# A fused attention and feed-forward block on one core: where the queries are turned, where an inverse root is taken, and who adds the first groups

## The chip, the cores and the metric

The kernel runs on one NeuronCore of a Trainium2 chip. The metric is the device time of one execution in microseconds (us); lower is better. A core has a matrix engine (TensorE, PE in the rows; its weight loads are PEld), VectorE (DVE), ScalarE (ACT), GpSimd (POOL) and SyncE (SP), which here issues every DMA. The engines run their own instruction streams in order and meet only at semaphores. All DMAs of this kernel are served by the same 16 DMA engines.

## What is computed

```python
x = L0_attn_x                       # (4, 512, 1024) float32: 2048 tokens of 1024
xn = layernorm(x)                   # (x - mean) / sqrt(var + 1e-5)
q, k, v = (xn @ W.T + b).reshape(B, S, 32, 32)        # Wq, Wk, Wv
scores = einsum('bshd,bsgd->bshg', q, k) / sqrt(32)   # head against head, inside a token
scores = where(scores > 0.001, scores, -inf)
attn = softmax(scores) ; ctx = einsum('bshg,bsgd->bshd', attn, v)
x + (ctx @ Wo.T + bo) + ffn(xn)
# ffn: group-scaled int4 weights, gate and up 3584 x 1024, down 1024 x 3584, a scale per 128 inputs
```

Attention is not over the sequence: each token has its own 32 x 32 matrix of scores between its 32 heads.

## The kernel before

**Splitting in two.** Float32 values are held as two float16 parts, HI and LO, and a product is three float16 matmuls (two in the feed-forward part). ScalarE makes the HI part, VectorE or GpSimd the LO part.

**Attention.** The 2048 tokens are 16 tiles of 128. `opening` turns the weights of q, k and v on TensorE and projects tile 0 in between. Then `tile_2(i)` runs for i = 1 to 16 (`TT`). It has 24 quarters. In quarter s, `project(i, s)` does six 128x512 matmuls of tile i (unit s // 4: Q takes units 0 and 1, K 2 and 3, V 4 and 5), and the table `STEPS` hangs other pieces on: S0 to S3 are the scores of tile i-1, X the split of the normed input of tile i+1, V0 to V3 the products with V of tile i-1, and R0 to R3 (`batch`) turn the queries of tile i on TensorE, 32 transposes in four batches of eight, each copied out of PSUM by VectorE or ScalarE (`batch_copy`).

Each engine walks the same quarters in its own order. VectorE's for a tile is: statistics of the next input tile (quarter 0), `layer_norm` (quarter 2), `unit_copy` of unit 0 and `softmax_shift` (quarter 3), `x_part` (4), `unit_copy` of unit 1, mask, sum and division of the softmax (7), and the rest. ScalarE takes the square root of the variance between its copies of S2 and S3 (`ROOT_AT`). SyncE's order, all of it DMAs, is: load the next x, store the context, store V to DRAM (`store_v`), turn V from DRAM (`turn_v`), turn the next x (`turn_x`), turn the probabilities in four pieces (`turn_probs`), store the turned x (`store_xt`), turn K in two halves (`turn_k`).

**The last tile** (i = 16) projects nothing. Its quarters turn Wo on TensorE (`turn_wo`, 16 half rows through PSUM bank 1), start the output projection (`output_unit`, 12 matmuls a quarter into bank 0, emptied by ScalarE's `output_out` before the next), and do the scores and products of tile 15. The other 21 output units follow.

**Feed-forward.** 28 tiles t of 128 rows. A tile has 32 units idx (gate 0 to 15, up 16 to 31; group g = idx // 2 % 8, half = idx % 2), each four 128x512 matmuls into one of three pairs of PSUM banks. ScalarE scales the first group into the sum, VectorE scales and adds the seven others (`add_group`). Down units are woven in from tile 1's second half on.

Of the kernel before, what the change touches and what calls it, by code (L numbers as in the profile page):

```python
# [29 lines left out]
F32 = mybir.dt.float32  # L30
# [11 lines left out]
def build(nc, x_in, Wq, bq, Wk, bk, Wv, bv, Wo, bo, gate_q, gate_s, up_q, up_s, down_q, down_s, out):  # L42
# [24 lines left out]
    ctx_dram = nc.dram_tensor("ctx_scratch", [TT, P, TG, 2, KT, GROUPS], F16).ap()  # L67
    v_dram = nc.dram_tensor("v_scratch", [P, NH * P], F16).ap()
    xt_dram = nc.dram_tensor("xt_scratch", [TT, P, 2, KT, P], F16).ap()

    with ExitStack() as whole:
# [85 lines left out]
        ln_std = sem("ln_std")  # L157
        ln_rstd = sem("ln_rstd")
# [9 lines left out]
        k_turned = [sem(f"k_turned{k}") for k in range(2)]  # L168
        v_stored = sem("v_stored")
        v_turned = sem("v_turned")  # L170
        p_turned = [sem(f"p_turned{k}") for k in range(4)]
        batch_done = sem("batch_done")
        batch_out = [sem("batch_out_act"), sem("batch_out_dve")]
# [29 lines left out]
        gu_added = sem("gu_added")  # L203
        silu_done = sem("silu_done")
# [13 lines left out]
        def anchor(eng):  # L218
# [17 lines left out]
        STATS_AT, ROOT_AT, NORM_AT, SHIFT_AT, EXP_AT, MASK_AT, DIVIDE_AT, P_AT = 0, 2, 2, 3, 5, 7, 7, 8  # L236
# [14 lines left out]
        BATCH_AT = {17: 0, 19: 1, 21: 2, 23: 3}  # L251
        BIAS_AT = {10: 0, 13: 1, 15: 2}
        STATS_1, ROOT_1, NORM_1, X_1 = 10, 11, 12, 13
# [32 lines left out]
        def wo_bank():  # L286
            return psum[:, 1, :].rearrange("p (k r) -> p k r", r=P)

        def output_bank(n):
            return n % 2 if n > KT else 0  # L290

        def projects(i):
            return not (isinstance(i, int) and i == TT)

# [5 lines left out]

        BATCH_BANK = 2
# [15 lines left out]

        def batch_bank(m):
            return psum[:, BATCH_BANK + m % 2, :].bitcast(F16)

# [26 lines left out]

        def batch_dest(eng, j, m):

            wait_pos(eng, s_done, j * 4)  # L350
            return turned[:, Q, :].rearrange("p (t x) -> p t x", x=NH)\
                [:, :, 8 * m:8 * m + 8]

        def batch_source(m):
            return batch_bank(m).rearrange("p (x t) -> p t x", t=P)

# [68 lines left out]

        def adds_made(t, slot):

            before = (0, 28)[t] if isinstance(t, int) and t < 2 else 32 * t - 6  # L430
            return before + sum(in_use(t, n) and not is_first(t, n) for n in range(slot + 1))
# [56 lines left out]

        def h_part(t, half, part):
            return h_flat[:, bass.ds((t % 2) * (4 * HALF) + (half * 2 + part) * HALF, HALF)]  # L490
# [11 lines left out]
        def _(pe):  # L502
# [32 lines left out]
            def batch(j, m):  # L535

                if m == 0:
                    pe.wait_ge(unit_lo, j * 6 + (2 * Q + 2))

                if m < 2:  # L540
                    wait_pos(pe, batch_out[m], j * (1, 3)[m])
                else:
                    pe.wait_ge(batch_out[1], j * 3 + (m - 1))
                for n in range(8):
                    last = turn(batch_bank(m)[:, n * P:(n + 1) * P], stacks[:, Q, 8 * m + n, :], ident16[:])  # L545
                last.then_inc(batch_done, 1)

            def scores(j, k):

                if k == 0:  # L550

                    pe.wait_ge(batch_out[0], j + 1)
                    pe.wait_ge(batch_out[1], j * 3 + 3)
# [28 lines left out]
            def first_quarter(s):  # L582
# [4 lines left out]
                if s in BATCH_AT:  # L587

                    pe.wait_ge(w_hi, 3 * KT)
                    pe.wait_ge(w_lo, 3 * KT)  # L590
                    batch(0, BATCH_AT[s])

            def turn_wo(n2):
# [3 lines left out]
                if n2 == 0:  # L597

                    pe.wait_ge(unit_copied, TT * 6)
                else:  # L600
                    pe.wait_ge(wo_hi, n2)
                    pe.wait_ge(wo_lo, n2)
                for k in range(4):
                    last = turn(psum[:, 1, k * P:(k + 1) * P],
# [3 lines left out]
            def output_unit(n, ks):  # L608

                c, ho = n // KT, n % KT  # L610
                if ks[0] == 0:
# [6 lines left out]
                    if n and n != KT + 1:  # L618

                        pe.wait_ge(proj_out, n if n <= KT else n - 1)  # L620
# [8 lines left out]
            def tile_2(i):  # L629
                for s in range(QUARTERS):  # L630
                    if projects(i):
                        project(i, s)
                    else:
                        if s < 2 * KT:
                            turn_wo(s)
                        if s >= 2:
                            output_unit(s // 2 - 1, range(4 * (s % 2), 4 * (s % 2) + 4))
                    for kind, n in steps_of(i, s):
                        if kind == "R":
                            batch(i, n)  # L640
                        elif kind == "S":
                            scores(i - 1, n)
                        elif kind == "V":
                            head_products(i - 1, n)

# [9 lines left out]
            def pair_free(t, slot):  # L655
# [6 lines left out]
                if is_first(tile_of, before):  # L662
                    mat, _, half = unit_of(tile_of, SLOTS[before][1])
                    pe.wait_ge(gu_first, firsts_made(tile_of, mat, half))
                else:
# [104 lines left out]
        def _(act):  # L770
# [10 lines left out]
            def root(i):  # L781
                act.wait_ge(ln_var, i + 1)
                run(ln_small[:, 3:4], ln_small[:, 2:3], ACT.Sqrt).then_inc(ln_std, 1)

# [6 lines left out]
            def unit_part(i, u):  # L791
# [3 lines left out]
                if u // 2 == Q:  # L795
                    wait_pos(act, batch_done, i * 4)
# [6 lines left out]

            def batch_copy(j, m):
                act.wait_ge(batch_done, j * 4 + (m + 1))
                dst = batch_dest(act, j, m)
                run(dst, batch_source(m), ACT.Copy).then_inc(batch_out[0], 1)
# [753 lines left out]
```

## Time and profile before

| | |
|---|---|
| median of 3 runs | 2034.37 us (2034.3 to 2034.48) |
| the profiled execution | 2035.56 us, its span 2033.8 us |
| granted TensorE clock over the span | 0.998 |
| busy: PE, DVE, ACT, POOL | 97%, 77%, 60%, 67% of the span |
| attention tiles | 72 to 624 us |
| last tile, with the start of the output projection | 624 to 698.5 us |
| rest of the output projection | 698.5 to 816 us |
| feed-forward | 816 us to the end |

The profiled execution's time is its span and 1.8 us around it. It lies 1.2 us above the median of the runs.

### The profile page before, as it was taken

The numbers are of one execution on the slowest core, as the hardware profiler recorded it, in microseconds if no ns is written. First come the engines' busy times: TensorE is split into PE (matmuls) and PEld (weight loads), VectorE is DVE, ScalarE is ACT, GpSimd is POOL, SyncE is SP. The second block draws the span as 40 slices with busy tenths as digits, with TensorE's granted clock in tenths as the row PEclk, the third lists the DMA queues.
The fourth block names the chain that finished last, engine by engine and source line by source line (L and its number), as shares of the span: only waits on it lengthen the run. The fifth ranks groups of instructions, "written<-read, shape, count | busy, mean of one in ns | idle before, by whom it ended". The sixth has DMA issues, their size and how long they took to land.

```text
span 2033.8 us, 35912 instructions
## 1 busy us (share of the span) xinstructions
PE 1979.7 (97%) x10368; PEld 945.0 (46%) x10368; DVE 1569.9 (77%) x1565; ACT 1211.0 (60%) x1967; POOL 1354.9 (67%) x772
## 2 busy tenths in 40 slices
PE   7999999999998999899999999999999999999997
PEld 5555555555554444244444444444444444444444
DVE  6667667777674200899999999999999999999997
ACT  5577777777765211356665656666566666666663
POOL 1445646555462000168888988888888988889888
PEclk9999999999999999999999999999999999999999
DMA  9676776777766462112221212212122121221236
GB/s 299 165 178 155 178 180 153 181 174 164 178 145 187 98 250 63 47 47 52 55 79 46 52 46 62 72 46 52 46 66 68 46 52 49 74 57 47 51 109 248
DMA packets 398870, 219.51 MB, mean 108 GB/s; under 512 B 335985, under 2 KB 372849, under 8 KB 396785
## 3 DMA queue, kind: packets, MB, share of 16 engines
q1 hardware_dynamic: 398832, 219.02, 41.4%
q8 instruction: 23, 0.38, 0.1%
q14 instruction: 15, 0.11, 0.0%
HBM read 96.29 MB, written 41.94 MB: 68 GB/s over the span
## 4 chain that ended last, share of the span: by engine, by line
PE 63%; issue 15%; POOL 12%; DVE 6%; DMA 2%; ACT 1%; SPq 1%; DVEq 0%; POOLq 0%; ACTq 0%
PE banks L677 34%; PE banks L702 16%; POOL stacks L1201 9%; PE banks L623 8%; DVE lower L1143 6%; PE banks L529 4%; POOL p_stack L1201 3%; DMA w_rows<-in_L_attn_Wv_dram 1%; POOL acc L1243 1%; PE banks L513 0%; PE banks L735 0%; SPq L1324 0%; PE banks L578 0%; ACT acc L854 0%; PE banks L545 0%
## 5 line engine op out<-in xcount | busy, mean ns | idle before, releaser
L677 PE MATMUL banks<-xt,lower 128*128 128x512 f16 x3584 | 857.2, 379 | 14.0 <-DVE lower L1143 9.2
L1243 POOL TENSOR_TENSOR acc<-acc,lower 128x1024 f32<-128x1024 f32 x326 | 766.9, 2364 | 144.6 <-ACT lower L961 144.6
L961 ACT ACTIVATE lower<-banks,down_scale 128x512 f32<-128x512 f32 x652 | 412.8, 684 | 366.9 <-PE banks L702 284.4
L1143 DVE SCALAR_TENSOR_TENSOR lower<-banks,gate_scale,lower 128x1024 f32<-128x1024 f32 x392 | 479.7, 1277 | 143.5 <-PE banks L677 143.2
L677 PEld LDWEIGHTS banks<-xt,lower 128*128 128x128 f16 x3584 | 343.3, 98 | 459.2 <-DVE lower L1143 74.9
L529 PE MATMUL banks<-wt,xt_tile 128*128 128x512 f16 x2304 | 527.4, 379 | 0.9 <-DMA xt_tile<-x_parts 0.9
L1143 DVE SCALAR_TENSOR_TENSOR lower<-banks,up_scale,lower 128x1024 f32<-128x1024 f32 x392 | 480.0, 1277 | 27.4 <-PE banks L677 23.6
L702 PE MATMUL banks<-lower 128*128 (+1 forms) x1792 | 458.8, 379 | 1.0 <-ACT lower L961 0.6
L1201 POOL TENSOR_TENSOR stacks<-unit,stacks 128x512 f16<-128x512 f32 x192 | 246.9, 1310 | 271.5 <-ACT stacks L801 271.5
L529 PEld LDWEIGHTS banks<-wt,xt_tile 128*128 (+1 forms) x2304 | 218.0, 98 | 229.4 <-issue 1.1
L702 PEld LDWEIGHTS banks<-lower 128*128 (+1 forms) x1792 | 171.0, 98 | 217.6 <-ACT lower L961 11.2
L1249 POOL TENSOR_TENSOR lower<-lower 128x1024 f32<-128x1024 f32 x56 | 132.4, 2365 | 189.7 <-DVE lower L1143 189.7
L623 PE MATMUL banks<-lower 128*128 128x512 f16 x768 | 170.4, 381 | 3.3 <-ACT acc L854 3.3
L1155 DVE SCALAR_TENSOR_TENSOR acc<-banks,down_scale,acc 128x1024 f32<-128x1024 f32 x106 | 135.6, 1279 | 28.5 <-PE banks L702 28.4
L1069 DVE TENSOR_TENSOR ctx_parts<-banks,ctx_parts 32x256 f16<-32x256 f32 x256 | 107.6, 420 | 58.2 <-ACT ctx_parts L840 55.1
L801 ACT ACTIVATE stacks<-unit 128x512 f16<-128x512 f32 x192 | 110.0, 620 | 62.7 <-DVE unit L1033 62.1
L1201 POOL TENSOR_TENSOR p_stack<-p_c,p_stack 128x256 f16<-128x256 f32 x128 | 81.2, 672 | 61.6 <-ACT p_stack L831 61.6
L1253 POOL TENSOR_TENSOR lower<-lower 128x1024 f32 (+1 forms) x56 | 119.6, 2136 | 2.1 <-ACT lower L948 2.1
L840 ACT ACTIVATE ctx_parts<-banks 32x256 f16<-32x256 f32 x256 | 96.0, 375 | 40.2 <-PE banks L578 35.7
L623 PEld LDWEIGHTS banks<-lower 128*128 128x128 f16 x768 | 75.0, 98 | 92.4 <-issue 7.1
L817 ACT ACTIVATE s_c<-banks 32x256 f32<-32x256 f32 x256 | 96.0, 375 | 7.2 <-PE banks L562 3.6
L934 ACT ACTIVATE lower<-banks,up_scale 128x1024 f32<-128x1024 f32 x56 | 62.4, 1114 | 49.6 <-PE banks L677 49.6
(55 smaller groups left out, 1178.3 us busy)
## 6 DMA issues: line engine op xcount, KB each, us to landing
v_scratch<-stacks SPq DMA_DIRECT2D x16, 1024.0 KB, 3.9
lower<-in_L_ffn_gate_q_dram SPq DMA_DIRECT2D x28, 512.0 KB, 3.7
lower<-in_L_ffn_up_q_dram SPq DMA_DIRECT2D x28, 512.0 KB, 4.5
lower<-in_L_ffn_down_q_dram SPq DMA_DIRECT2D x28, 512.0 KB, 4.0
x_tile<-in_L_attn_x_dram SPq DMA_DIRECT2D x16, 512.0 KB, 3.9
xt_scratch<-xt_tile SPq DMA_DIRECT2D x16, 512.0 KB, 3.1
ctx_scratch<-ctx_parts SPq DMA_DIRECT2D x64, 128.0 KB, 2.1
lower<-ctx_scratch SPq DMA_DIRECT2D x4, 2048.0 KB, 8.6
```

Source lines behind the costliest of these rows:

```text
L529: last = mm(psum[:, u % 2, :], xt_tile[:, :, :].rearrange("p a b -> p (a b)")[:, bass.ds(at, P)], wt[:, u // 2, wp, k, (u % 2) * BANK:(u % ...
L623: last = mm(psum[:, output_bank(n), :], wo_t[:, wp, k, ho * P:(ho + 1) * P], ctx_t[c % 2][:, :, cp, k, :], start=(k == 0 and m == 0), stop ...
L677: last = mm(psum[:, 2 * (slot % 3) + c, :], gu_t[:, mat, g, :], xt[:, (2 * half + c) * CT:(2 * half + c + 1) * CT, part, g, :], start=(par ...
L702: last = mm(psum[:, bank, :], weights[:, bass.ds((t % 2) * (KT * P) + ho * P, P)], h_flat[:, bass.ds(at, BANK)], start=(part == HI), stop= ...
L801: last = run(dst[n], src, ACT.Copy)
L961: run(down_tmp[:, buffer, c * BANK:(c + 1) * BANK], psum[:, 6 + c, :], ACT.Copy, scale=scale)\
L1143: v.scalar_tensor_tensor(out=acc_of[:, half, :], in0=gu_pair(slot % 3), scalar=scale[:, :, :].rearrange("p t k -> p (t k)")[:, bass.ds(t * ...
L1155: v.scalar_tensor_tensor(out=acc[:, half, ho, :], in0=gu_pair(slot % 3), scalar=down_scale[:, :, :].rearrange("p h t -> p (h t)")[:, bass. ...
L1201: return g.tensor_tensor(dst, src, hi, ALU.subtract)
L1243: g.tensor_tensor(acc[:, half, ho, :], acc[:, half, ho, :], down_tmp[:, buffer, :], ALU.add).then_inc(down_added, 1)
L1249: g.tensor_tensor(h_sb[:, half, :], h_sb[:, half, :], u_acc[:, half, :], ALU.mult).then_inc(h_done, 1)
L1253: g.tensor_tensor(h_part(t, half, LO), h_sb[:, half, :], h_part(t, half, HI), ALU.subtract)\
```

## The change

Four edits:

1. **Queries.** R0 to R3, their PSUM banks and their copies go. The two halves of the queries' stack are stored to DRAM by SyncE (`store_q`, before the probabilities are turned), and one DMA transpose per tile brings all of it back turned (`turn_queries`, after the probabilities and before K). `store_xt` moves behind `turn_k`.
2. **Root.** ScalarE's Sqrt and VectorE's reciprocal go. VectorE takes the inverse root by a guess on the bits and four Newton steps of three instructions each, inside `layer_stats`.
3. **Output projection.** `turn_wo` alternates between banks 3 and 1 and runs one half row ahead, the first at the end of tile 15; `output_unit` alternates between banks 0 and 2; SyncE loads the third row block of Wo before it turns V.
4. **Spare adds.** In feed-forward tile 0 the groups 2 and 5, and in tile 1 the group 4 of the gate, are no longer scaled and added by VectorE: ScalarE scales them out of PSUM (`spare_copy`), and GpSimd adds them up (`spare_total`, `spare_add`).

```diff
-        STEPS = [["S0"], ["S1"], ["S2"], ["S3"], ["X"], [], [], [], [], [], [], [], [], ["R0"],
-                 ["R1"], ["R2"], ["R3", "V0"], ["V1"], [], ["V2"], ["V3"], [], [], []]
+        STEPS = [["S0"], ["S1"], ["S2"], ["S3"], ["X"], [], [], [], [], [], [], [], [], [],
+                 [], [], ["V0"], ["V1"], [], ["V2"], ["V3"], [], [], []]
...
+            def inverse_root(i):
+                var, root, t = ln_small[:, 2:3], ln_small[:, 4:5], ln_small[:, 3:4]
+
+                dve.wait_ge(ln_var, i + 1)
+                v.tensor_scalar(root.bitcast(I32), var.bitcast(I32), -0.5, float(ROOT_GUESS), ALU.mult, ALU.add)\
+                    .then_inc(ln_guess, 1)
+                dve.wait_ge(ln_guess, i + 1)
+                for n in range(ROOT_STEPS):
+
+                    v.scalar_tensor_tensor(out=t, in0=root, scalar=var, in1=root, op0=ALU.mult, op1=ALU.mult)\
+                        .then_inc(ln_square, 1)
+                    dve.wait_ge(ln_square, i * ROOT_STEPS + (n + 1))
+                    v.tensor_scalar(t, t, -0.5, 1.5, ALU.mult, ALU.add).then_inc(ln_factor, 1)
+                    dve.wait_ge(ln_factor, i * ROOT_STEPS + (n + 1))
+                    v.tensor_tensor(root, root, t, ALU.mult).then_inc(ln_root, 1)
+                    dve.wait_ge(ln_root, i * ROOT_STEPS + (n + 1))
...
-        def wo_bank():
-            return psum[:, 1, :].rearrange("p (k r) -> p k r", r=P)
+        def wo_bank(n2):
+            return psum[:, 3 - 2 * (n2 % 2), :]
...
         def output_bank(n):
-            return n % 2 if n > KT else 0
+            return 2 * (n % 2)
...
+        SPARE = ((4, 5, 10, 11, 20, 21, 26, 27), (8, 9))
...
+            def store_q(i):
+                wait_pos(sp, q_turned, i * 16)
+                anchor(sp)
+                for half in range(2):
+                    sp.wait_ge(unit_lo, i * 6 + (2 * Q + 1 + half))
+                    anchor(sp)
+                    at = slice(half * (NH // 2), (half + 1) * (NH // 2))
+                    sp.dma_start(q_dram.rearrange("t (x c) -> t x c", c=4 * DH)[:, at, :], stacks[:, Q, at, :])\
+                        .then_inc(q_stored[half], 16)
+
+            def turn_queries(i):
+
+                if isinstance(i, int) and i == 0:
+                    sp.wait_ge(w_turned, 3 * KT)
+                for half in range(2):
+                    sp.wait_ge(q_stored[half], i * 16 + 16)
+                    anchor(sp)
+                wait_pos(sp, s_done, i * 4)
+                anchor(sp)
+                sp.dma_start_transpose(turned[:, Q, :], q_dram.rearrange("t (x c) -> (t x) c", c=4 * DH))\
+                    .then_inc(q_turned, 16)
...
                 store_v(i - 1)
+                if not projects(i):
+                    load_wo(2)
                 turn_v(i - 1)
...
+                if projects(i):
+                    store_q(i)
                 for q in range(4):
                     turn_probs(i - 1, q)
+                if projects(i):
+                    turn_queries(i)
+                    turn_k(i)
                 if not isinstance(i, int) or i + 1 < TT:
                     store_xt(i + 1)
-                if projects(i):
-                    turn_k(i)
```

SyncE's DMAs of one attention tile, from the load of the next x on, before:

```order
L1310 DMA x_tile<-in_L_attn_x_dram 128x1024
L1366 DMA v_scratch<-stacks 128x4096
L1373 DMA_TRANSPOSE turned<-v_scratch 128x4096
L1324 DMA_TRANSPOSE xt_tile<-x_parts 128x16x128
L1397 DMA_TRANSPOSE probs_t<-p_stack 128x8x128 x4
L1331 DMA xt_scratch<-xt_tile 128x2048
L1386 DMA_TRANSPOSE turned<-stacks 128x16x128 x2
```

And the same tile of the change:

```order
L1345 DMA x_tile<-in_L_attn_x_dram 128x1024
L1401 DMA v_scratch<-stacks 128x4096
L1408 DMA_TRANSPOSE turned<-v_scratch 128x4096
L1359 DMA_TRANSPOSE xt_tile<-x_parts 128x16x128
L1418 DMA q_scratch<-stacks 128x2048 x2
L1454 DMA_TRANSPOSE probs_t<-p_stack 128x8x128 x4
L1430 DMA_TRANSPOSE turned<-q_scratch 128x4096
L1443 DMA_TRANSPOSE turned<-stacks 128x16x128 x2
L1366 DMA xt_scratch<-xt_tile 128x2048
```

Two stores stand ahead of the probabilities, the queries' transpose stands ahead of K's two, and the next load of x stands behind all of them.

VectorE, from the statistics of the next input tile on, before:

```order
L1003 BN_AGGR ln_small<-stats 128x2
L1005 TENSOR_SCALAR ln_small<-ln_small 128x1
L1009 RECIPROCAL ln_small<-ln_small 128x1
L1011 TENSOR_SCALAR x_tile<-x_tile,ln_small 128x1024
L1033 SCALAR_TENSOR_TENSOR unit<-banks,bias_qkv 128x512
L1047 TENSOR_REDUCE sums<-s_c 128x32
L1051 TENSOR_TENSOR p_c<-s_c,sums 128x1024
```

And the change; of the four Newton steps the first is shown, and three more such triples follow before `layer_norm`, `unit_copy` and the maximum of the scores:

```order
L1002 BN_AGGR ln_small<-stats 128x2
L1004 TENSOR_SCALAR ln_small<-ln_small 128x1
L1011 TENSOR_SCALAR ln_small<-ln_small 128x1
L1016 SCALAR_TENSOR_TENSOR ln_small<-ln_small 128x1
L1019 TENSOR_SCALAR ln_small<-ln_small 128x1
L1021 TENSOR_TENSOR ln_small<-ln_small 128x1
```

One instruction and a wait on ScalarE gave way to thirteen small instructions, in the same place ahead of the softmax.

## Rows read from the trace of the kernel before

**Rows 1.** Busy time by stage: window, its length, busy us of each engine, clock, DMA share, GB/s.

```profile
72.00:624.00 552.00, 547.52 (x3594) 291.04 (x3591) 384.88 (x563) 399.36 (x864) 308.59 (x300) 1.00 0.72 170
624.00:698.50 74.50, 63.84 (x356) 33.76 (x357) 21.82 (x33) 29.63 (x64) 7.34 (x10) 0.95 0.47 136
816.00:872.84 56.84, 47.59 (x197) 16.68 (x197) 49.38 (x42) 15.68 (x16) 6.80 (x3) 1.00 0.16 42
```

**Rows 2.** PE in time: start, us; S0 of three tiles, and one batch of the queries.

```profile
329.49 0.61 PE L562 MATMUL banks<-turned 128*128 128x128 f16 x8
...
348.57 1.46 PE L529 MATMUL banks<-wt,xt_tile 128*128 128x512 f16 x6
...
349.87 0.61 PE L545 MATMUL banks<-ident,stacks 128*128 128x128 f16 x8
...
350.31 1.46 PE L529 MATMUL banks<-wt,xt_tile 128*128 128x512 f16 x6
...
587.45 0.61 PE L562 MATMUL banks<-turned 128*128 128x128 f16 x8
```

**Rows 3.** SyncE's queue in time: when DMAs are issued, and how long issuing took.

```profile
350.75 5.51 SPq L1397 DMA_TRANSPOSE probs_t<-p_stack  x4
356.60 0.37 SPq L1331 DMA_DIRECT2D xt_scratch<-xt_tile  x1
357.32 5.15 SPq L1386 DMA_TRANSPOSE turned<-stacks  x2
363.02 0.40 SPq L1310 DMA_DIRECT2D x_tile<-in_L_attn_x_dram  x1
```

**Rows 4.** Busy time by window; the last two numbers are DMA share and GB/s.

```profile
333.90:336.50 2.60, 2.60 (x20) 1.42 (x19) 0.00 (x0) 2.55 (x5) 0.00 (x0) 1.00 0.97 400
338.60:342.60 4.00, 4.00 (x20) 1.84 (x19) 3.97 (x3) 3.92 (x5) 2.72 (x2) 1.00 1.16 260
347.40:351.70 4.30, 4.30 (x35) 2.45 (x33) 3.89 (x4) 3.21 (x10) 2.41 (x4) 1.00 0.00 0
351.70:357.40 5.70, 5.46 (x50) 3.37 (x49) 2.84 (x6) 4.75 (x11) 5.70 (x8) 1.00 0.95 180
357.40:359.10 1.70, 1.70 (x12) 0.81 (x10) 1.63 (x5) 0.70 (x2) 1.42 (x2) 1.00 1.02 324
359.10:364.10 5.00, 5.00 (x37) 2.72 (x35) 3.40 (x8) 4.15 (x10) 1.70 (x2) 1.00 1.14 210
```

**Rows 5.** Time to landing of K's second half (360.5:362) and of x (363:364).

```profile
turned<-stacks SPq DMA_TRANSPOSE x1, 4.3
...
x_tile<-in_L_attn_x_dram SPq DMA_DIRECT2D x1, 512.0 KB, 3.6
```

**Rows 6.** VectorE in time, with the idle time before an instruction and what ended it.

```profile
330.04 1.29 DVE L1000 BATCH_NORM_STATS2 stats<-x_tile 128x6 f32<-128x512 f32 x2 [0.52 <-DMA x_tile<-in_L_attn_x_dram]
...
331.73 0.15 DVE L1005 TENSOR_SCALAR ln_small<-ln_small 128x1 f32<-128x1 f32 x1
336.93 0.16 DVE L1009 RECIPROCAL ln_small<-ln_small 128x1 f32<-128x1 f32 x1 [5.05 <-ACT ln_small L783]
337.13 0.81 DVE L1011 TENSOR_SCALAR x_tile<-x_tile,ln_small 128x1024 f32<-128x1024 f32 x1
...
338.49 1.22 DVE L1047 TENSOR_REDUCE sums<-s_c 128x32 f32<-128x1024 f32 x1
```

**Rows 7.** ScalarE in time, ahead of the square root of the variance.

```profile
335.40 1.28 ACT L783 ACT_TABLE_LOAD   x1
```

**Rows 8.** PE in time: the last tile.

```profile
640.69 1.11 PE L604 MATMUL banks<-ident,lower 128*128 128x128 f32 x4 [4.81 <-DMA lower<-in_L_attn_Wo_dram]
...
649.84 2.75 PE L623 MATMUL banks<-lower 128*128 128x512 f16 x12 [0.43 <-ACT acc L854]
```

**Rows 9.** VectorE and ScalarE in time: feed-forward tile 0.

```profile
819.47 16.81 DVE L1143 SCALAR_TENSOR_TENSOR lower<-banks,gate_scale,lower 128x1024 f32<-128x1024 f32 x14 [117.47 <-PE banks L677]
...
817.15 2.12 ACT L934 ACTIVATE lower<-banks,gate_scale 128x1024 f32<-128x1024 f32 x2 [1.21 <-PE banks L677]
```

More of the change, by code:

```diff
@@ L168, in build @@
         k_turned = [sem(f"k_turned{k}") for k in range(2)]
+        q_stored = [sem(f"q_stored{k}") for k in range(2)]
+        q_turned = sem("q_turned")
         v_stored = sem("v_stored")
@@ L426, in units_made, with by_spare, spares_made @@
             return before + sum(in_use(t, n) for n in range(slot + 1))
+        SPARE = ((4, 5, 10, 11, 20, 21, 26, 27), (8, 9))
+        def by_spare(t, kind, unit):
+            return kind == "gu" and isinstance(t, int) and t < 2 and unit in SPARE[t]
+        def spares_made(t, unit):
+            return t * len(SPARE[0]) + SPARE[t].index(unit) + 1
         def adds_made(t, slot):
-            before = (0, 28)[t] if isinstance(t, int) and t < 2 else 32 * t - 6
-            return before + sum(in_use(t, n) and not is_first(t, n) for n in range(slot + 1))
+            before = (0, 20)[t] if isinstance(t, int) and t < 2 else 32 * t - 16
+            return before + sum(in_use(t, n) and not is_first(t, n) and not by_spare(t, *SLOTS[n]) for n in range(slot + 1))
         def has_prev(t):
@@ L533, in project @@
                     last.then_inc(unit_done, 1)
[L535 to L546, printed above, removed]
             def scores(j, k):
                 if k == 0:
-                    pe.wait_ge(batch_out[0], j + 1)
-                    pe.wait_ge(batch_out[1], j * 3 + 3)
+                    pe.wait_ge(q_turned, j * 16 + 16)
                     pe.wait_ge(k_turned[0], j * 16 + 16)
@@ L644, in tile_2 @@
                             head_products(i - 1, n)
+                if ends(i):
+                    turn_wo(0)
             def first_tile():
@@ L874, in tile_2 @@
                             head_products_hi(i - 1, n)
-                    if s == ROOT_AT and (not isinstance(i, int) or i + 1 < TT):
-                        root(i + 1)
                     if s == EXP_AT:
@@ L1161, in tile @@
                 for idx in range(32):
-                    if unit_of(t, idx)[1]:
+                    if unit_of(t, idx)[1] and not by_spare(t, "gu", idx):
                         add_group(t, idx)
@@ L1260, in tile @@
                             add_down(12 * (t - back) + slow_rank(d), d // 8, d % 8)
+                    if not has_prev(t) and idx in (11, 27):
+                        for half in range(2):
+                            spare_total(idx // 16, half)
+                    if isinstance(t, int) and (t, idx) in ((0, 15), (0, 31), (1, 15)):
+                        for half in range(2):
+                            spare_add(t, idx // 16, half)
                     if idx in POOL_AT and has_prev(t):
```

149 lines of the change are left out of this document (85 added, 64 removed).

## The prediction

> **What bounds the kernel now.** I read the stages first [rows 1]. In the attention tiles PE is busy 547.5 of 552 us: a PE-bound stage. But its DMA share is 0.72, so the question for a change that moves PE work into DMAs is when in a tile those DMAs run. The last tile has 10.7 us of idle PE and a clock of 0.95. The first feed-forward stretch has 9.2 us of idle PE with VectorE busy 49.4 of 56.8: VectorE-bound.
>
> Then one attention tile in time. S0 comes at 329.49 and, seven tiles later, at 587.45: a tile takes 257.96 / 7 = 36.85 us [rows 2]. A batch of the queries costs the step from 349.87 to 350.31, 0.44 us; six matmuls before it take 349.87 - 348.57 = 1.30, 0.216 each.
>
> Then SyncE's queue. The first probability transpose is issued at 350.75, x_t's store at 356.60, K's halves from 357.32, and the load of the next x only at 363.02, since the issues of K are held up [rows 3]. The DMA windows say why: from 351.7 to 364.1 the 16 engines have a share of 0.95 to 1.14 without a gap; probabilities 5.7 us, the store 1.7, K 5.0, and x behind them [rows 4]. K's second half is issued at 360.5 and lands 4.3 later, at 364.9; x at 363.0 plus 3.6 = 366.6 [rows 5]. S0 of the next tile is due at 329.49 + 36.85 = 366.34. So K has 1.4 us to spare, and x lands 15.9 us behind the first probability transpose. **That DMA queue is nearly a bound of its own.**
>
> Last, VectorE, which works in order. The statistics start when x has landed (330.04), the variance is there at 331.88, and it idles 5.05 us for ScalarE's root, then norm, unit copy, and the maximum of the scores at 338.49 [rows 6]. From that maximum to the first probability transpose are 350.75 - 338.49 = 12.26 us.
>
> **The queries (edit 1).** Gone from PE: 4 x 0.44 = 1.8 us a tile; a tile bound by PE alone would take 35.05. Gone too are three copies of 1.2 us on VectorE and one of 1 us on ScalarE, which wait for nothing here and gain nothing. Added: two stores ahead of the probabilities, 1 MB together. V's store of the same size takes 2.6 us at 400 GB/s [rows 4]; the share is 0.00 from 347.4 to 351.7, ahead of the probabilities [rows 4], so I take them as hidden. If they were late they would push the probabilities by up to 2.6.
>
> Added after the probabilities: the transpose of the whole stack. Its twin is V's, same shape, from DRAM: 4.0 us at a share of 1.16 [rows 4]. The engines are full there, so K and everything behind moves by the full 4.0; I add 0.3 for its start behind the last probability piece. From below, a transpose could overlap what is in flight: bound 2.6, as a plain megabyte; from above 5.0, K's two halves of the same bytes. I take the twin.
>
> The Trainium skill has a rule that would change this term: "Advanced Engine Details and Errata", section "X-Bar Transpose (TRN2)", says that on this chip transposing DMAs are as fast as regular ones. This trace disagrees (260 and 210 GB/s against 400 for a plain store) [rows 4]. By the page the term would be 2.6, and the total below 1.4 x 14 = 20 us less.
>
> The move of `store_xt` behind K lets K land 1.7 earlier than it would, but x, behind both, gains nothing from it.
>
> **The root (edit 2).** ScalarE's table load of 1.28 and root leave the way between S2's and S3's copies [rows 7], and the exp needs no reload; that would bring the softmax about 1.4 us forward if the scores were what it waits for. VectorE gets 13 dependent instructions on 128x1. One such step is 336.93 to 337.13, 0.20 us [rows 6]: 2.6 us. From below 0.15 each (the busy time alone) is 2.0, from above 0.25 is 3.25. In the old schedule this fits into the 5.05 us of idle time. Whether it still does depends on when x lands.
>
> **Together they close a loop that does not contain PE.** From the first probability transpose of a tile: 15.9 us until x has landed, as before, plus 4.0 + 0.3 for the queries; statistics 1.85; root 2.6; norm and unit copy 338.49 - 337.13 = 1.4; from the maximum to the next first probability transpose 12.25. Sum: 15.9 + 4.3 + 1.85 + 2.6 + 1.4 + 12.25 = **38.3 us per tile**, against 36.85. K lands 14.1 + 4.3 - 1.7 = 16.7 behind the first probability transpose and lets S0 go, x lands 20.2 behind it: 3.5 after S0, where it was 330.04 - 329.49 = 0.55 [rows 2, 6]. The maximum then comes 3.5 + 1.85 + 2.6 + 1.4 = 9.3 after S0 (9.0 before), so it is VectorE's way that it waits for, not the scores. PE then has 3.2 us of waits a tile: at V0 for the probabilities and at S0 for K.
>
> Fourteen tiles (1 to 14) load a next x: 14 x (38.3 - 36.85) = **+20.3 us**.
>
> The opening loses its four batches, -1.8, and the first root, 2.6 instead of the 0.6 or so that root and reciprocal take, delays the first x transpose; I take 0.7 of it as seen. **-1.1 us.**
>
> **Output projection (edit 3).** Before, from S0 at 587.45 to the end of quarter 20 at 698.5, 111.0 us. Now tile 15 has no x: its first probability transpose comes about 18.7 after S0 (350.75 - 329.49 = 21.3 before, less 1.4 for the root and 1.2 for VectorE's split of x), K's packets end 16 later (5.7 + 0.3 + 4.0 + 5.0 and 1.1 of start) at 34.8. Wo's first rows, 512 KB, are queued behind K: 1.5 and landing, 37.0, where PE would ask for them at about 34: the first `turn_wo` is late. Wo's second rows and 2 MB of context (1.5 + 5.9 us at the plain rate) end at 43.7, landed at 44.4: the first output quarter waits for that. Context and V stores and Wo's third rows (1.5 + 2.6 + 1.6) are there at 50. Two quarters and their extras later, at 56.5, quarter 5 starts. From there 16 quarters of 2.59, ten turns of 0.43 and four V groups of 0.45 are 47.6, with neither the waits of 0.43 and more for ScalarE at the single bank nor their restarts [rows 8]: 104.1. I leave the cost of one stretch at half clock in, 1.75 as before. 105.9: **-5 us**, of which the banks are nearly all, since the DMA queue eats what the earlier load of Wo gives.
>
> **Spare adds (edit 4).** VectorE's adds come every 16.81 / 14 = 1.20 us, a unit needs 4 x 0.216 = 0.86 on PE [rows 9]. Three 16-unit stretches are VectorE-bound, 18.9 us each; at PE's pace they would be 13.8. But ScalarE's copy starts 1.15 after the unit's start and takes 1.1, and there are three PSUM pairs, of which the unused down slots skip one twice per stretch; a run of four or six adds still backs up. Walking the units through with these numbers I get 16.6, 17.9 and 17.9: **-3.6 us**. Bounds: 0 and -11.
>
> Sum: +20.3 - 1.1 - 5 - 3.6 = +10.6. The profiled execution lies 1.2 above the median, and since the sum is a difference I put it on the median: 2034.4 + 10.6 = **2045 us**.
>
> **Rivals.**
>
> *The queue has room after all.* If the queries' transpose costs 2.6 or less behind the probabilities, the tile takes 36.9 and the other edits win: 14 x 0.05 - 9.7 = -9, 2025. The sign turns at a tile of 37.5 us, a transpose of 3.2. Against it: no window in [rows 4] shows transposes faster than 260 GB/s. Chance 0.12.
>
> *The scores' loop, not x's.* If VectorE's small instructions overlap to almost nothing, or x lands earlier, the loop runs over K: 16.7 to K landed, and 21.3 - 1.4 = 19.9 from S0 to the next first transpose: 36.6. Total 14 x (-0.25) - 9.7 = -13, 2021. For it: x's landing is one arrow among many. Against: the queue's order is fixed. 0.1.
>
> *All hidden, PE-bound.* 14 x (-1.8) - 9.7 = -35, 2000. This is the other side's strongest form, and one mechanism: the DMA queue catches up in its idle stretches. But the queries, K and x have one order, and none can move ahead of the probabilities. 0.08.
>
> *PE's waits cost clock.* The last tile, with a wait of 4.81 at its longest, was granted 0.95 [rows 1, 8]; 3.2 us of waits in every tile might do it too. The stretch at half clock there was about 0.05 x 74.5 / 0.5 = 7.5 us, 3.7 us of work; a tile would take 35.05 + 3.7 = 38.8 or more, 2052 and up. 0.08.
>
> My forecast, a loop of 37.6 to 39.2 over x: 0.62. Its own range is 2036 to 2057.
>
> Another rule of the skill speaks against the whole edit: "VectorE: DVE Perf Modes", section "Rules for kernel authors", advises TensorE for a 128x128 transpose whose result may go to PSUM, and DMA otherwise. Here a block costs 0.44 / 8 = 0.055 us on PE and 4.0 / 32 = 0.125 us in the DMA queue; the trace agrees in direction.
>
> **Range and chances.** The range takes in the first two rivals' nearer parts and the clock's: 2024 to 2057. A measurement here tells 0.2% (4 us) from no change. Faster by more: 0.25, the first three rivals but for their middle; within: 0.13; slower by more: 0.62.
>
> **What would show it.** Right: S0 38.3 us apart; DMA share near 1 from the first probability piece to x; VectorE idle before the statistics, and the maximum right behind the unit copy; PE waiting at V0 and S0 for DMAs. The output stage without waits for ScalarE in bank 0. Feed-forward tile 0 some 2.5 us shorter. Wrong: S0 under 37 us apart, a gap between the queries' and K's transfers, or the maximum waiting for S3's copy. What would make it wrong is above all the 4.0 and the 0.20, each multiplied by 14.

## The result and the profile after

The changed kernel takes 2066.5 us (median of 6 runs, 2063.75 to 2068.77) against 2034.34 (6 runs), a ratio of 1.016 (95% interval 1.0147 to 1.0173). It is slower, as forecast, but by 32 us instead of 11, beyond the range. Its profiled span is 2061.9 us, 28.1 more than before; of the other 4 us, 2.8 come from the profiled execution being the fastest of the six, and 1.2 from that of before lying above its median.

By stage the two spans differ as follows. S0 of tile 0 (in `tile_2(1)`) comes at 70.52 instead of 71.82 (-1.3). The 14 tiles after it take 555.1 instead of 515.6 (+39.5): 39.65 each instead of 36.83. From the S0 behind them, tile 14's, to the end of quarter 20 of the last tile it is 104.8 instead of 111.05 (-6.2), the rest of the output projection is the same, the first feed-forward stretch takes 53.07 instead of 56.84 (-3.8). So one stage pays for everything.

Busy time by window of the changed kernel: length, busy us of PE, PEld, DVE, ACT, POOL, then clock, DMA share, GB/s. The rows answer to [rows 1].

```profile
70.00:625.00 555.00, 506.04 (x2911) 253.27 (x2912) 341.22 (x658) 323.91 (x754) 287.97 (x280) 0.97 0.85 211
625.00:730.50 105.50, 97.06 (x562) 52.44 (x560) 40.56 (x62) 51.66 (x117) 26.93 (x30) 0.97 0.67 184
847.95:901.02 53.07, 45.83 (x197) 17.50 (x198) 37.86 (x32) 26.59 (x26) 25.44 (x12) 1.00 0.18 45
```

The attention tiles are no longer PE-bound: PE idles 49 of 555 us, and the DMA share rose from 0.72 to 0.85. What it waits for in 70 to 625 us (total us, times, longest):

```profile
PE banks L572 <- DMA probs_t<-p_stack: 42.4, 14, 3.7
PE banks L556 <- DMA turned<-stacks: 7.4, 6, 2.0
```

PE's waits name the probabilities and K. What sets the pace is seen only by following one tile in time (start, us; in brackets the idle time before and its end):

```profile
348.13 0.61 PE L556 MATMUL banks<-turned 128*128 128x128 f16 x8
...
351.32 1.29 DVE L999 BATCH_NORM_STATS2 stats<-x_tile 128x6 f32<-128x512 f32 x2 [3.18 <-DMA x_tile<-in_L_attn_x_dram]
...
353.38 0.22 DVE L1016 SCALAR_TENSOR_TENSOR ln_small<-ln_small 128x1 f32<-128x1 f32 x1
353.63 0.15 DVE L1019 TENSOR_SCALAR ln_small<-ln_small 128x1 f32<-128x1 f32 x1
353.82 0.16 DVE L1021 TENSOR_TENSOR ln_small<-ln_small 128x1 f32<-128x1 f32 x1
354.02 0.22 DVE L1016 SCALAR_TENSOR_TENSOR ln_small<-ln_small 128x1 f32<-128x1 f32 x1
...
356.02 0.81 DVE L1026 TENSOR_SCALAR x_tile<-x_tile,ln_small 128x1024 f32<-128x1024 f32 x1
...
357.35 1.21 DVE L1057 TENSOR_REDUCE sums<-s_c 128x32 f32<-128x1024 f32 x1
...
369.61 5.53 SPq L1454 DMA_TRANSPOSE probs_t<-p_stack  x4
373.05 0.61 PE L572 MATMUL banks<-probs_t,turned 128*128 128x128 f16 x8 [2.25 <-DMA probs_t<-p_stack]
375.52 4.07 SPq L1430 DMA_TRANSPOSE turned<-q_scratch  x1
379.83 4.79 SPq L1443 DMA_TRANSPOSE turned<-stacks  x2
...
385.87 0.36 SPq L1345 DMA_DIRECT2D x_tile<-in_L_attn_x_dram  x1
386.59 1.93 SPq L1392 DMA_DIRECT2D ctx_scratch<-ctx_parts  x4
386.88 0.62 PE L556 MATMUL banks<-turned 128*128 128x128 f16 x8 [1.52 <-DMA turned<-stacks]
...
391.43 0.69 DVE L999 BATCH_NORM_STATS2 stats<-x_tile 128x6 f32<-128x512 f32 x1 [6.21 <-DMA x_tile<-in_L_attn_x_dram]
```

The maximum (357.35) follows norm and unit copy with no wait, though the scores began 9.2 us before; 12.26 later the first probability transpose is issued; x has landed and its statistics start 21.8 after that. That is the loop over x: transpose, DMA queue, x, statistics, root, norm, maximum, next transpose. The DMA windows behind the issue at 369.61, in the columns of [rows 1]:

```profile
376.50:380.90 4.40, 4.40 (x34) 2.48 (x33) 3.76 (x10) 2.83 (x8) 1.16 (x2) 1.00 1.13 237
380.90:385.90 5.00, 4.46 (x21) 1.84 (x19) 3.22 (x7) 2.43 (x7) 2.27 (x2) 1.00 1.09 205
385.90:387.70 1.80, 0.82 (x10) 0.66 (x11) 0.00 (x0) 0.66 (x2) 1.22 (x2) 1.00 1.03 339
387.70:391.00 3.30, 3.30 (x29) 1.97 (x27) 0.00 (x0) 2.84 (x8) 1.05 (x1) 1.00 0.94 310
```

Queries 4.4, K 5.0, the store of x_t 1.8, and then 3.3 us in which x shares the engines with the context, whose stores are issued 0.7 us behind it.

### The profile page after: what moved, and what is told of

The parts are those of the page before. It is cut to its first block, busy times and chain, and to the rows that moved or that the text cites. A ratio compares the mean times of both kernels' runs of the same rounds, so it can differ in the third digit from the quotient of the medians.

```text
span 2061.9 us, 35046 instructions
## 1 busy us (share of the span) xinstructions
PE 1968.6 (95%) x9856; PEld 926.8 (45%) x9856; DVE 1534.2 (74%) x1699; ACT 1166.0 (57%) x1918; POOL 1377.0 (67%) x782
## 4 chain that ended last, share of the span: by engine, by line
PE 59%; issue 16%; POOL 12%; DVE 7%; SPq 2%; DMA 2%; ACT 1%; DVEq 0%; POOLq 0%; ACTq 0%
PE banks L671 34%; PE banks L696 16%; POOL stacks L1212 9%; PE banks L615 8%; DVE lower L1154 5%; POOL p_stack L1212 3%; PE banks L537 1%; POOL acc L1254 1%; SPq L1443 0%; DMA lower<-in_L_attn_Wo_dram 0%; SPq L1430 0%; DMA x_tile<-in_L_attn_x_dram 0%; PE banks L521 0%; DMA probs_t<-p_stack 0%; PE banks L729 0%
## 5 line engine op out<-in xcount | busy, mean ns | idle before, releaser
L1154 DVE SCALAR_TENSOR_TENSOR lower<-banks,gate_scale,lower 128x1024 f32<-128x1024 f32 x386 | 472.8, 1277 | 147.7 <-PE banks L671 147.4
L537 PE MATMUL banks<-wt,xt_tile 128*128 128x512 f16 x2304 | 533.3, 386 | 0.0
L537 PEld LDWEIGHTS banks<-wt,xt_tile 128*128 (+1 forms) x2304 | 223.3, 99 | 247.1 <-issue 12.2
L1262 POOL TENSOR_TENSOR lower<-lower 128x1024 f32<-128x1024 f32 x56 | 132.6, 2367 | 0.0
L1267 POOL TENSOR_TENSOR lower<-lower 128x1024 f32<-128x1024 f32 x4 | 9.3, 2356 | 167.9 <-ACT lower L927 167.9
```

Of the source, the lines that this page charges most:

```text
L537: last = mm(psum[:, u % 2, :], xt_tile[:, :, :].rearrange("p a b -> p (a b)")[:, bass.ds(at, P)], wt[:, u // 2, wp, k, (u % 2) * BANK:(u % ...
L1154: v.scalar_tensor_tensor(out=acc_of[:, half, :], in0=gu_pair(slot % 3), scalar=scale[:, :, :].rearrange("p t k -> p (t k)")[:, bass.ds(t * ...
L1262: g.tensor_tensor(h_sb[:, half, :], h_sb[:, half, :], u_acc[:, half, :], ALU.mult).then_inc(h_done, 1)
```

## Experiments

The loops' pieces, for every kernel: means over the first 13 tiles of its profiled execution, in us, worked out from the timelines' start times. I is the issue of the first probability transpose, "stats" the start of the statistics, "max" that of the maximum of the scores.

| kernel | tile | I to stats | stats to max | max to I | I to S0 |
|---|---|---|---|---|---|
| before | 36.83 | 16.32 | 8.21 | 12.26 | 15.69 |
| the change | 39.66 | 21.42 | 6.02 | 12.26 | 17.26 |
| e1, x early | 37.85 | 15.76 | 8.60 | 13.08 | 17.13 |
| e2, queries on PE | 36.45 | 16.39 | 7.16 | 12.80 | 16.18 |
| e3, half the queries | 37.69 | 19.31 | 6.11 | 12.26 | 16.39 |
| e4, eight steps | 42.36 | 21.62 | 8.58 | 12.26 | 17.28 |
| e5, context late | 39.29 | 20.94 | 6.03 | 12.26 | 17.41 |
| e6, before + root | 36.45 | 16.41 | 7.18 | 12.81 | 16.14 |
| e7, old root | 38.38 | 21.63 | 4.44 | 12.27 | 17.19 |
| e8, banks + adds | 36.81 | 16.25 | 8.25 | 12.26 | 15.67 |
| e9, queries first | 44.26 | 16.77 | 7.43 | 19.83 | 16.19 |

The three middle columns follow one another from one I to the next, so they sum to about a tile in every row, waits included; whether the loop over x binds shows only in what the maximum waits for. "stats to max" and "max to I" are taken over tiles 0 to 12, "I to stats" and "I to S0" lead on to tiles 1 to 13.

A warning on single numbers: the change, e1, e3, e5 and e9 have the same opening, and their S0 of tile 0 comes at 70.52, 74.13, 72.56, 71.93 and 71.38. Differences of up to 3.6 us in the opening of one trace say nothing about an edit.

My theory was: the queries' transpose and the Newton steps together close a loop through x's landing, without PE. The rival: x is one arrow among many, and something else (the DMA queue's volume, PE's waits and clock, K) sets the pace.

**e1_x_early: x taken out of the loop.**

```diff
-                if not isinstance(i, int) or i + 1 < TT:
-                    load_x(i + 1)
...
                     turn_x(i + 1)
+                if not isinstance(i, int) or i + 2 < TT:
+                    load_x(i + 2)
```

> The changed kernel with one thing moved: SyncE issues the load of the x after next right behind the turn of the next x, ahead of the stores of the queries, instead of at the end of the DMA queue of a tile (the last loop iteration is peeled off so that the row index stays in range). My theory: the tile's 39.65 us are the loop first probability transpose, DMA queue, x landed, statistics, root, softmax, first probability transpose. With x landed early, the maximum of the scores waits for ScalarE's copy of S3 (7.5 us after S0), the first probability transpose comes 7.5 + 12.3 = 19.8 after S0, and S0 of the next tile 17.3 after that, as measured: 37.1 us a tile, 14 x 2.55 = 36 us less in all, about 2031. Rival A, the DMA queue's total of bytes sets the pace wherever x stands: 39 us or more a tile, no change. Rival B, the half clock in PE's waits sets it: little change, since a wait at V0 remains.

Measured 2043.57 us (1.0042, 1.0028 to 1.0056 of before): 23 us of the 32 are back, by this move alone. The gain is 12.6 short of what I expected. VectorE, PE and SyncE in one tile of e1:

```profile
337.94 1.27 DVE L1000 BATCH_NORM_STATS2 stats<-x_tile 128x6 f32<-128x512 f32 x2
...
339.00 0.62 PE L557 MATMUL banks<-turned 128*128 128x128 f16 x8 [0.85 <-DMA turned<-stacks]
...
346.46 1.22 DVE L1058 TENSOR_REDUCE sums<-s_c 128x32 f32<-128x1024 f32 x1 [1.22 <-ACT s_c L803]
...
359.62 5.50 SPq L1455 DMA_TRANSPOSE probs_t<-p_stack  x4
```

The statistics now run before S0, and the maximum waits for ScalarE's copy of the scores, 7.46 after S0: the second loop, over scores, probabilities, queries and K. It sums to 7.46 + 13.08 + 17.13 = 37.7, where I had 37.1: the way from maximum to I is 0.8 longer than in the kernel before. In single tiles it is either 12.27 or 13.15; e1 has the longer way from tile 1 on, e2 and e6 in seven or eight of 13 tiles. The traces show the piece that differs: VectorE's instruction behind the maximum, which subtracts it, took 2.20 us beside GpSimd's, and 1.22 in the change:

```profile
310.25 3.25 POOL L1213 TENSOR_TENSOR stacks<-unit,stacks 128x512 f16<-128x512 f32 x2 [6.36 <-ACT stacks L792]
310.29 2.20 DVE L1062 TENSOR_TENSOR p_c<-s_c,sums 128x1024 f32<-128x1024 f32 x1
...
358.59 1.22 DVE L1061 TENSOR_TENSOR p_c<-s_c,sums 128x1024 f32<-128x1024 f32 x1
358.78 4.17 POOL L1212 TENSOR_TENSOR stacks<-unit,stacks 128x512 f16<-128x512 f32 x2 [7.10 <-ACT stacks L791]
```

The first two lines are of e1, the last two of the change. In all eleven traces it took 2.20 whenever GpSimd's instruction had started first (54 times, by 0.03 to 0.04 us), and 1.22 whenever GpSimd's started after it (111 times, by 0.02 to 0.19). That it is the order of the two starts is read off the traces; no run moved it on purpose.

**e2_pe_queries: the change with the queries on TensorE.** R0 to R3, `batch` and `batch_copy` as before, `store_q` and `turn_queries` gone; root, banks and spare adds stay.

```diff
-        STEPS = [["S0"], ["S1"], ["S2"], ["S3"], ["X"], [], [], [], [], [], [], [], [], [],
-                 [], [], ["V0"], ["V1"], [], ["V2"], ["V3"], [], [], []]
+        STEPS = [["S0"], ["S1"], ["S2"], ["S3"], ["X"], [], [], [], [], [], [], [], [], ["R0"],
+                 ["R1"], ["R2"], ["R3", "V0"], ["V1"], [], ["V2"], ["V3"], [], [], []]
```

> The changed kernel with the queries' edit undone: TensorE turns them in four batches again, no store and no DMA transpose of them, the store of the turned x ahead of K as before. Newton's root, the output projection's banks and the spare adds stay. My theory: attention tiles back to 36.85 us (VectorE's 2.9 us of root fits into its 5 us of idle time), the output stage shorter by 6 to 10 us than before (no queries in the queue ahead of Wo), feed-forward 3.8 shorter: 2034.3 minus 10 to 14, 2020 to 2024. A rival in which Newton's root costs by itself: tiles over 36.9, nearer 2030 or above.

Measured 2017.74 us (0.9915, 0.9898 to 0.9931), 2.3 under the lower end of what I expected. Without edit 1 the change is a gain; with it, a loss of 32. Edit 1 costs 2066.5 - 2017.7 = 48.8 us in this company. The tiles take 36.45 each and not the 36.85 of my theory, all alike to 0.01, with PE busy without a gap; e6 says where the 0.4 come from.

**e3_half_q: half of the disputed transfer.** `turn_queries` moves only the first 64 tokens' queries from tile 1 on; the others keep tile 0's values, so this kernel is for its time alone.

```diff
+                some = P if isinstance(i, int) and i == 0 else P // 2
-                sp.dma_start_transpose(turned[:, Q, :], q_dram.rearrange("t (x c) -> (t x) c", c=4 * DH))\
+                sp.dma_start_transpose(turned[:, Q, :some * NH],
+                                       q_dram[:some, :].rearrange("t (x c) -> (t x) c", c=4 * DH))\
```

> The changed kernel, but from tile 1 on only the first 64 tokens' queries are turned (half of the DMA transpose; the other half of the queries keeps tile 0's values). My theory, a serial queue: half of 4.3 us gone from the loop, 37.5 us a tile, 14 x 2.15 = 30 us less, 2036. Rival, in which the transpose is not what delays x but the stores and their writes to DRAM: under 1 us a tile less, 2055 or above.

One run, 2036.83 us, where I expected 2036; I to statistics fell by 2.1, half of the 4.3. The tile came down with it, 39.66 to 37.69: time in the queue behind the probabilities is paid nearly one for one, 2.0 of 2.1 us.

**e4_newton8: the other term doubled.** `ROOT_STEPS` is 8.

> The changed kernel with eight Newton steps in place of four. My theory: VectorE's root lies in the loop, a step costs 0.22 + 0.15 + 0.16 with gaps, 0.64 us as measured, so four more cost 2.55 a tile, 42.2, and 14 x 2.55 = 36 us in all, 2102. If the loop is closed elsewhere (DMA bytes or K), VectorE has idle time and nothing changes: 2066.

One run, 2106.74 us, 4.7 above what I expected, with S0 of tile 0 at 75.26, 4.7 later than in the change, and a tile of 42.36 where I had 42.2. In this kernel's tile whose S0 is at 371.35 the statistics start at 374.86, and:

```profile
382.12 0.81 DVE L1026 TENSOR_SCALAR x_tile<-x_tile,ln_small 128x1024 f32<-128x1024 f32 x1
383.44 1.21 DVE L1057 TENSOR_REDUCE sums<-s_c 128x32 f32<-128x1024 f32 x1
```

8.58 us from statistics to maximum instead of 6.02: four steps cost 2.56, 0.64 each, and 14 tiles all show it. VectorE's smallest instructions are on the path that sets the time, although VectorE is busy only 341 of 555 us in the change.

**e5_context_late: is x's transfer stretched by the context?**

```diff
-                if not isinstance(i, int) or i > 1:
-                    store_context(i - 2)
                 store_v(i - 1)
...
                     turn_x(i + 1)
+                if not isinstance(i, int) or i > 1:
+                    store_context(i - 2)
```

> The changed kernel, with the store of the context moved from right behind the load of the next x to behind the turn of the next x. Theory (the next x lands last in a loop over the DMA queue, and its transfer of 2.3 us is stretched to 3.3 because the context's packets are mixed into it): each of 14 tiles takes 39.65 - 1.0 = 38.65 us, and the whole 2066.5 - 14 = 2052.5 us, with x's packets in 2.3 us again. Rival (x's transfer is stretched by its own reads of the input, or by what is still in the queue from K and the store of x_t): no change, 2066 us.

Measured 2063.18 us (4 runs, 2063.11 to 2063.8). From the issue of x to the statistics it is 4.63 us instead of 5.33, so the context's packets do stretch x. But the issue of the queries' transpose moved back by 0.15 behind I, K's and x's by 0.2, and S0 of tile 0 came 1.4 later; of the 14 us I expected 3.3 are left. Partly right: 0.5 us of I to statistics was the context.

**e6_root_alone: the kernel before with edit 2 alone.**

> The kernel before with the root edit alone: four Newton steps on VectorE in place of Sqrt and reciprocal. Theory (there the 13 small instructions fit into VectorE's idle time, and the table loads leave the way from the scores to the softmax): the maximum comes at 7.5 us after S0 instead of 9.0, V0 no longer waits for the probabilities, a tile takes 36.45 instead of 36.85, 2034.4 - 5.5 = 2029 us. Rival (the 0.4 us a tile come from another edit; the root is hidden either way): 2034 us.

Measured 2028.16 us (0.9968, 0.9956 to 0.998), tiles 36.45, as expected. VectorE and PE in time, and the stage's window:

```profile
327.28 0.61 PE L566 MATMUL banks<-turned 128*128 128x128 f16 x8
...
334.78 1.22 DVE L1058 TENSOR_REDUCE sums<-s_c 128x32 f32<-128x1024 f32 x1 [0.46 <-ACT s_c L817]
```
```profile
72.00:624.00 552.00, 548.05 (x3621) 293.21 (x3622) 435.60 (x734) 367.28 (x835) 303.53 (x302) 1.00 0.74 173
```

The maximum waits for ScalarE's last copy (0.46 here, 0.07 in six of 14 tiles), 7.5 after S0 instead of 9.0 [rows 2, 6]: the root is off VectorE's path, and the table load off ScalarE's. The kernel before has two table loads a tile, ahead of the root and ahead of the exponentials; in e6 and in the change both are gone.

**e7_old_root: the change without edit 2.** Sqrt and reciprocal are back.

```diff
+            def root(i):
+                act.wait_ge(ln_var, i + 1)
+                run(ln_small[:, 3:4], ln_small[:, 2:3], ACT.Sqrt).then_inc(ln_std, 1)
...
-                inverse_root(i)
```

> The changed kernel with the square root back on ScalarE and the reciprocal on VectorE. Theory (the loop over x is closed by the queries' transpose alone; the root only adds the difference between 2.87 us of Newton and about 1.9 of table load, root and reciprocal): a tile takes 38.6 to 38.9 us, against 39.65; 2051 to 2056 us. Rival (the Newton steps are what brings VectorE onto the path; with Sqrt the queries' transpose is hidden): a tile near 36.9, about 2026 us.

Measured 2045.64 us (1.0047, 1.0032 to 1.0063): 21 less than the change, and 5 less than I expected at the least. ScalarE, PE and VectorE in one tile:

```profile
379.98 0.62 PE L553 MATMUL banks<-turned 128*128 128x128 f16 x8 [1.77 <-DMA turned<-stacks]
```
```profile
384.13 1.53 ACT L803 ACTIVATE s_c<-banks 32x256 f32<-32x256 f32 x4 [0.21 <-PE banks L553]
385.68 1.28 ACT L774 ACT_TABLE_LOAD   x1
386.17 0.15 DVE L1011 TENSOR_SCALAR ln_small<-ln_small 128x1 f32<-128x1 f32 x1
386.97 0.20 ACT L774 ACTIVATE ln_small<-ln_small 128x1 f32<-128x1 f32 x1
387.20 1.53 ACT L803 ACTIVATE s_c<-banks 32x256 f32<-32x256 f32 x4
```
```profile
388.76 1.22 DVE L1048 TENSOR_REDUCE sums<-s_c 128x32 f32<-128x1024 f32 x1
```

Load and root stand in front of S3's copy, which ends at 388.73; the maximum starts there, at 8.78 after S0 in 12 of 14 tiles. The binding loop is now the one over the scores: 8.78 + 12.27 + 17.19 = 38.2. x's stands close behind it: the variance is there at 386.32, and the root, which has its place behind S2's copy and the load, starts 0.65 later; in eleven of the twelve tiles x has 0.3 to 0.9 us to spare in this way, in one 1.8. Neither theory had this: the queries' transpose alone makes two loops, both longer than PE's 36.8, one of 38.2 over the scores and one some 0.6 shorter over x, and the Newton steps shorten the first and lengthen the second.

**e8_banks_adds: the kernel before with edits 3 and 4 alone.**

> The kernel before with the output projection's banks and the spare adds alone (queries on TensorE, Sqrt on ScalarE). Theory (the parts add up where the queries stay on TensorE: all three gave 2017.7, the root alone 2028.2 of 2034.8): 2034.8 - (2028.2 - 2017.7) = 2024.3 us, tiles at 36.85 us as before. Rival (the output stage gained only because the root had left the last tile's softmax way): 2027 us or more.

Measured 2022.11 us (0.9937, 0.9924 to 0.9951), tiles 36.81, 2.2 under what I expected. The parts add up to within 2.3 us, which is inside the intervals: 2034.3 - 2022.1 = 12.2 for edits 3 and 4, and 4.4 more for the root on top of them, against 6.7 for it alone. Behind S0 of tile 14 this kernel's span is 12.5 us shorter than before, the change's only 10.1: PE waits there 2.2 us in all for DMAs of Wo, and in the change 8.2 for Wo and the context, which have the last queries and K ahead of them in the queue.

**e9_q_first: the queries' transpose in the DMA engines' idle time.** e1, with `turn_queries` ahead of `turn_probs` and V0 to V3 two quarters later.

```diff
+                if projects(i):
+                    turn_queries(i)
                 for q in range(4):
                     turn_probs(i - 1, q)
                 if projects(i):
-                    turn_queries(i)
                     turn_k(i)
```

> The kernel with the early load of x (2043.6 us), with the queries' transpose ahead of the probabilities, where the DMA engines idle, and V0 to V3 two quarters later, so that PE does not wait for the later probabilities. Theory (then only K's way closes a loop: 19.4 us from S0 until the queries' second store has landed, 4.3 and 6.7 for queries and probabilities, 5.0 for K, 1.3 of starts and landing): a tile takes 36.7 us in place of 37.5, about 2032 us. Rival (the later products with V hold up the next tile's scores at the PSUM banks they share): 37.8 us or more a tile, 2045 us and up.

Measured 2128.71 us (1.0463, 1.0447 to 1.0479), a tile 44.3. The theory missed by 97 us; the rival's "2045 and up" holds the number, but its mechanism is the small part of it. SyncE's queue, PE, and the window behind the queries' stores:

```profile
352.46 0.84 SPq L1346 DMA_DIRECT2D x_tile<-in_L_attn_x_dram  x1
353.66 0.86 SPq L1419 DMA_DIRECT2D q_scratch<-stacks  x2
360.07 3.72 SPq L1431 DMA_TRANSPOSE turned<-q_scratch  x1
364.05 5.53 SPq L1455 DMA_TRANSPOSE probs_t<-p_stack  x4
```
```profile
367.52 1.01 PE L573 MATMUL banks<-probs_t,turned 128*128 128x128 f16 x8 [6.17 <-DMA probs_t<-p_stack]
```
```profile
355.00:358.50 3.50, 3.50 (x18) 1.58 (x17) 1.26 (x2) 3.41 (x10) 2.62 (x5) 1.00 0.99 372
```

There is no idle time behind the stores to use: issued at 353.66 to 354.52 behind x_t's transpose and x, they have landed only at 360.07, 5.5 us later and 24.0 us after S0, where I had taken 19.4. SyncE waits for them with the probabilities behind it, which go out 28 us after S0 instead of e1's 20.6, and PE stands 6.2 us at V0, 79.7 us in 13 tiles. What the rival named is there too, PE waiting at S0 for VectorE to empty the PSUM banks of the late products, but with 10.5 us in 13 tiles it is the lesser part.

## Why the prediction was wrong in size

**The mechanism was right.** The change is slower by a loop over the DMA queue, x's landing, statistics, Newton steps and softmax. e1 takes x out of it (-23 us, down to the next loop), e3 halves its queries' term, e4 lengthens its root's term, and the last two moved the tile by what the loop says. The traces also show what the prediction listed: maximum right behind the unit copy, PE waiting at V0 and S0 for DMAs (3.6 us a tile, 3.2 forecast), no gap between queries and K.

**The step that failed is the sum for the tile, 38.3 forecast and 39.65 measured, and in it above all the way from the first probability transpose until x has landed: 15.9 + 4.3 = 20.2 forecast, 21.4 measured.** In 14 tiles the sum's error is 18.9 us of the 21.5 missed. Part of those is in no stage: between the two profiled executions the change costs 28.1 us, not 32.2, and there the tiles are 19.2 over the forecast and the rest 1.6 under it. By the tile's parts, from the table (21.42 + 6.02 + 12.26):

- *15.9 from the first transpose to x landed.* That was one tile, the one in [rows 3 to 6]. The mean over 13 tiles of before is 16.32. 0.4 a tile, 6 us in all, came from taking a sample for a mean that the same trace had.
- *4.0 + 0.3 for the queries.* Its packets took 4.4 in the tile shown; the twin was the right row. The Trainium skill's rule in "Advanced Engine Details and Errata", section "X-Bar Transpose (TRN2)", that transposing DMAs are as fast as regular ones on this chip, is contradicted here too, with 237 GB/s in that window against 400 for V's store [rows 4]. But from I to statistics the loop grew by 5.1, not 4.3. The missing 0.8 was a term put at nothing: x's own transfer now comes when the context of the tile before is ready, whose stores are issued 0.7 us behind x instead of 2.8, and the two share the engines. e5 gives back 0.5 of it; where the other 0.3 go stays open.
- *1.85 + 2.6 + 1.4 from statistics to maximum.* 5.85 forecast, 6.02 measured: the root takes 2.87 (353.15 to 356.02), since the scalar_tensor_tensor step is 0.25 apart and not 0.20. 0.17 a tile, 2.4 us.
- *12.25 from maximum to first transpose:* 12.26, so the queries' stores ahead of the probabilities did stay hidden.

**The other terms came out near, not all by merit.** Opening -1.1, measured -1.3: with equal openings up to 3.6 us apart, that it agrees is luck. Spare adds -3.6, measured -3.8; but the three stretches that the forecast adds up (16.6, 17.9 and 17.9 for 18.9 each) give -4.3, so the number written down was nearer than its working. GpSimd's first sums appear and VectorE's adds come in runs of four instead of fourteen [rows 9]:

```profile
853.07 1.11 ACT L927 ACTIVATE lower<-banks,gate_scale 128x1024 f32<-128x1024 f32 x1 [1.85 <-PE banks L671]
...
855.88 4.86 DVE L1154 SCALAR_TENSOR_TENSOR lower<-banks,gate_scale,lower 128x1024 f32<-128x1024 f32 x4 [2.00 <-PE banks L671]
...
860.68 4.67 POOL L1267 TENSOR_TENSOR lower<-lower 128x1024 f32<-128x1024 f32 x2 [159.87 <-ACT lower L927]
```

Output projection 105.9 instead of 111.0, measured 104.8 instead of 111.05. Its waits stand where the prediction put them, on Wo's and the context's DMAs and no longer on bank 0 [rows 8]:

```profile
663.74 1.97 PE L596 MATMUL banks<-ident,lower 128*128 128x128 f32 x8 [4.57 <-DMA lower<-in_L_attn_Wo_dram]
...
671.03 2.75 PE L615 MATMUL banks<-lower 128*128 128x512 f16 x12 [1.88 <-DMA lower<-ctx_scratch]
```

**The rivals.** "The queue has room" and "all hidden" are out: queries, K and the store of x_t take their 4.4, 5.0 and 1.8 us one behind the other. "The scores' loop" is real but stands behind x's, and at 37.7 (e1), not 36.6. "PE's waits cost clock" is half true: the tiles were granted 0.97 instead of 1.00, in eleven stretches at 1.2 GHz, ten at V0 with waits of 2.2 to 3.7 us and one behind S0 with 2.0; four waits of 1.8 to 3.2 us at V0 had none. But PE was not what the loop waited for: the eleven tiles with such a stretch average 39.7 and the three without 39.4. A price of 0.3 us a tile at most is a comparison within one trace, and no run separates it.

**What the prediction saw by half** is how edits 1 and 2 meet. It had the root's 2.6 us in the loop over x, but gave edit 2 nothing of its own, and did not price the change without it. Alone it is worth -6.7 us (e6), 5.3 of them in 14 tiles, because with table load and root gone from ScalarE and off VectorE's wait the probabilities reach V0 in time (13 waits of at most 0.3 us before, none in e6). With edit 1, which makes x late, the same edit costs 2066.5 - 2045.6 = +20.9 us (e7): its 2.9 us of small instructions no longer fit into idle time. Edit 1 costs 2045.6 - 2022.1 = +23.5 us with the old root and 48.8 with the new one.

The best kernel of the study is e2, 2017.7 us, 0.8% under the kernel before. With the queries' transposes in this queue the best tile of a whole kernel was e1's 37.85 us, more than the 36.45 that PE needs with the queries on it; the 1.8 us of PE work that edit 1 removes was cheaper than the 4.3 us of queue that it adds.

## What to carry to other kernels

Before moving work from a busy engine to DMAs, follow the queue once round: if a tile's transfers are issued in one order and the last of them starts the next tile's softmax, that circle is a bound of its own, and while it is the longest, every microsecond put ahead of its last member counts in full, once per tile. Take that member out, and the next loop may stand just behind it. An edit that fits into an engine's idle time is free only while what feeds that engine is not late, so edits should be priced, and measured, in the company they will have. And take each term of a loop as a mean over tiles: half a microsecond in a sample tile is 7 us in fourteen.

## What the runs showed of the hardware

- A chain of dependent 128x1 instructions on VectorE costs 0.19 to 0.25 us a link with the semaphore between, though each is busy 0.15 to 0.22; a Newton step of three is 0.64 us (e4: four more, 2.56). In e1, where the first step ran beside GpSimd's TENSOR_TENSOR, two of its links took 0.51 and 0.93 in 13 of 16 tiles.
- A TENSOR_TENSOR of 128x1024 float32 on VectorE took 2.20 us when a TENSOR_TENSOR on GpSimd had started at most 0.04 us before it, and 1.22 when it came first (eleven traces, 54 and 111 times).
- The load of x, 512 KB, took the engines 2.2 us in the kernel before (its packets run from 364.1 to 366.3), and 3.3 in the change, where four 128 KB stores of the context are issued 0.7 us behind it: later transfers of this queue share the engines with an unfinished one (e5: 0.7 us less from issue to use when they are moved).
- Two 512 KB stores issued behind a transpose of x_t and a load of x landed 5.5 us after both were issued (e9), at an engine share of 0.99: here the wait for a store to land cost more than the 4.4 us of the transpose behind it.
- The same idle time of PE cost clock in one kernel and hardly any in another. In the 14 tiles e7 waited 45.8 us for DMAs, in two waits a tile with at most 1.9 us at V0; it had two stretches at 1.2 GHz, both at S0 with waits of 3.0 and 2.4, and its span was granted 0.994. The change waited 49.8 us, 42.4 of it at V0 with up to 3.7 at once; it had eleven, and was granted 0.988.
